# Sandwich block on one core: new per-engine orders of work, another assignment of PSUM banks, other waits

## The reference

```
q, k, v = LN(x) @ Wq.T + bq, LN(x) @ Wk.T + bk, LN(x) @ Wv.T + bv     # 16 heads of 8
q, k = exp(q), exp(k)
num = q . cumsum(k outer v);  den = sum(q * cumsum(k))
x1  = x + LN((num / den) @ Wo.T + bo)
xn  = rms_norm(LN(x1)) * gamma_x;  se = rms_norm(slot_embeds) * gamma_slot   # 512 slots
logits = xn @ se.T
slots  = softmax(logits over tokens).T @ xn
h      = gelu(slots @ w1) @ w2
out    = x1 + LN(softmax(logits over slots) @ h)
```

## Time and profile before

| | us |
|---|---|
| median of 3 runs | 595.33 (594.32 to 596.03) |
| profiled execution, its own time | 594.64 |
| span of the profile | 592.9 |
| PE busy (3772 matmuls) | 557.5, 94% |
| PE weight loads busy | 486.1, 82% |
| DVE busy | 484.2, 82% |
| ACT busy | 473.4, 80% |
| POOL busy | 473.1, 80% |
| mean granted TensorE clock | 0.984 of 2.4 GHz |

### The profile page before, as it was taken

How to read it: one execution, slowest core, us unless ns; L and a number is a source line. 1 busy time by engine, 2 the same in 40 slices (tenths; PEclk the granted TensorE clock), 3 DMA queues, 4 the chain that set the end, 5 groups by cost and what they waited for, 6 DMA issues and landing times.

```text
span 592.9 us, 10573 instructions
## 1 busy us (share of the span) xinstructions
PE 557.5 (94%) x3772; PEld 486.1 (82%) x3772; DVE 484.2 (82%) x922; ACT 473.4 (80%) x1244; POOL 473.1 (80%) x462
## 2 busy tenths in 40 slices
PE   7937999999999999999999999999999999999886
PEld 7925898888888898888888988888888988887775
DVE  4897888888988888888888888889888888878430
ACT  3255889988888889888888899888888888888663
POOL 4777888889888988889888888898888888974100
PEclk9958999999999999999999999999999999999999
DMA  4000000000000000000000000000000000000000
GB/s 115 10 19 19 19 9 19 19 28 28 27 28 28 10 28 18 28 28 28 28 27 28 10 26 20 28 28 28 28 27 12 26 19 28 19 26 10 11 9 19
DMA packets 16825, 14.29 MB, mean 24 GB/s; under 512 B 2850, under 2 KB 16644, under 8 KB 16772
## 3 DMA queue, kind: packets, MB, share of 16 engines
q1 hardware_dynamic: 14708, 12.76, 7.1%
q10 hardware_dynamic: 2064, 0.86, 0.6%
HBM read 5.25 MB, written 4.19 MB: 16 GB/s over the span
## 4 chain that ended last, share of the span: by engine, by line
PE 42%; POOL 23%; ACT 19%; DVE 10%; issue 3%; DMA 1%; SPq 0%; POOLq 0%; DVEq 0%; ACTq 0%
POOL kv_lo L318 11%; PE banks L929 9%; PE banks L955 8%; POOL x_rs L296 7%; ACT kv_hi L422 6%; ACT L430 6%; PE banks L802 5%; PE banks L804 5%; PE banks L803 5%; DVE prod L1253 4%; ACT hid L447 3%; DVE xh L1157 3%; PE banks L782 3%; PE banks L881 2%; ACT disp_t L545 2%
## 5 line engine op out<-in xcount | busy, mean ns | idle before, releaser
L942 PE MATMUL banks<-w_c,hid 128*128 128x128 f32 x1024 | 124.6, 276 | 2.4 <-ACT hid L447 2.4
L942 PEld LDWEIGHTS banks<-w_c,hid 128*128 128x128 f32 x1024 | 119.2, 192 | 3.5 <-ACT hid L447 2.2
L318 POOL TENSOR_TENSOR kv_lo<-kv,kv_hi 128x1152 fp32r<-128x1152 f32 x31 | 81.7, 2636 | 32.5 <-ACT kv_hi L422 32.5
L1253 DVE TENSOR_TENSOR prod<-banks,E 128x768 f32<-128x768 f32 x96 | 88.3, 948 | 1.9 <-PE banks L882 1.9
L1268 DVE TENSOR_REDUCE banks<-prod 128x288 f32<-128x2304 f32 x32 | 81.5, 2545 | 0.0
L212 POOL TENSOR_TENSOR kv_prev<-prev 128x1024 f32<-128x1024 f32 x31 | 66.8, 2153 | 10.5 <-DMA prev<-E 10.5
L955 PEld LDWEIGHTS banks<-proc,comb 128*128 128x128 f32 x512 | 61.1, 191 | 17.0 <-DVE prod L1253 14.9
L380 POOL TENSOR_TENSOR kv<-kv,kv_prev 128x1024 f32<-128x1024 f32 x31 | 74.7, 2410 | 0.0
L447 ACT ACTIVATE hid<-banks 128x512 f32<-128x512 f32 x128 | 70.5, 612 | 4.8 <-PE banks L804 2.0
L212 POOL TENSOR_TENSOR kv<-E 128x1024 f32<-128x1024 f32 x32 | 68.6, 2144 | 4.1 <-ACT E L422 2.2
L1318 DVE TENSOR_REDUCE neg_max<-banks 128x4 f32<-128x1024 f32 x32 | 39.2, 1224 | 31.2 <-PE banks L804 31.2
(11 more groups left out here) (140 smaller groups left out, 1516.9 us busy)
## 6 DMA issues: line engine op xcount, KB each, us to landing
X<-in_L_attn_x_dram SPq DMA_DIRECT2D x32, 128.0 KB, 2.1
out_dram<-res SPq DMA_DIRECT2D x32, 128.0 KB, 2.0
prev<-E SPq DMA_DIRECT2D x32, 112.0 KB, 2.1
w_in<-in_L_ffn_w_dram ACTq DMA_DIRECT2D x2, 256.0 KB, 4.6
prev<-E SPq DMA_DIRECT2D x32, 15.0 KB, 2.0
se_in<-n_L_ffn_slot_embeds_dram ACTq DMA_DIRECT2D x1, 256.0 KB, 3.2
w_in<-in_L_attn_Wq_dram SPq DMA_DIRECT2D x1, 64.0 KB, 2.4
w_in<-in_L_attn_Wk_dram SPq DMA_DIRECT2D x1, 64.0 KB, 2.2
```

The lines of the kernel that those rows point to most:

```text
L318: pool.tensor_tensor(kv_lo[:, :], kv[:, :], kv_hi[:, :].bitcast(F32), ALU.subtract)\
L942: last = pe.matmul(PR[:, j, :], hid[:, f, j * P:(j + 1) * P], w2_c[:, f, :], start=(f == 0), stop=(f == FJ - 1))
L1253: dve.tensor_tensor(prod[u][:, :, d0 * DIM:d1 * DIM].rearrange("p c (d f) -> p c d f", d=g), CU[k].rearrange("p (o d f) -> p o d f", o=1, ...
```

## The change

No operation is added or removed; the lists, the banks and the waits are new.

- **Banks.** The second and third unit of `cumulate` get banks 4 and 0, so no two units share one. The mixture's output moves to 4, the gathered slots to 6, the first transposed dispatch weights to 1, the attention transposes to 6. The four groups of `hidden` go to 5, 2, 5 and 0. Bank 2 is one of the two of the logits.
- **TensorE.** `subtract_max` comes ahead of `cumulate(.., 2)`, `att_transpose` ahead of `project`, `hidden` runs 0, 1, 3, 2. `logits(n)` now waits for gelu 1 of the block before, `project` for gelu 3.
- **SP's queue.** `shift_odd(s - 1)` is issued ahead of `store(s - 8)`.
- **VectorE.** `x_statistics` comes ahead of the two maxima, `x_normalise` ahead of `dispatch_scale`, both residuals behind it; `multiply` runs 2, 1, 0; `xT_low` and `own_sum` come later.
- **ScalarE.** `v_evict` comes ahead of `dispatch_exp`, `combine_exp(.., 0)` ahead of `dispatch_copy`, `slT_high` ahead of `xT_high`, `o_squares` between two gelus.
- **GpSimd.** `x_rstd_of` comes ahead of `sums_low` of the block before, `o_rstd_of` behind it.
- The first blocks are written out anew: `wo_centre` and `x_statistics(3)` come behind the first multiplies, `w2_centre` behind `xnT_high(0)`. PE's and DVE's regular step now reach into the tail.

The diff, cut to its core (of the lists, the regular steps alone):

```diff
@@ banks
-        CU = [banks[:, 6, 0:DU * DIM], banks[:, 5, 0:DU * DIM], banks[:, 5, 0:DU * DIM]]
+        CU = [banks[:, 5, 0:DU * DIM], banks[:, 4, 0:DU * DIM], banks[:, 0, 0:DU * DIM]]
-        AT = banks[:, 7, 0:SEQ]
-        YO = banks[:, 4, 0:NC * YW]
+        AT = banks[:, 6, 0:SEQ]
+        YO = banks[:, 6, 0:NC * YW]
-        DT = [banks[:, 0, :], banks[:, 7, :]]
-        SL = banks[:, 0, :]
-        HP = [banks[:, 6, :], banks[:, 0, :], banks[:, 6, :], banks[:, 4, :]]
+        DT = [banks[:, 1, :], banks[:, 7, :]]
+        SL = banks[:, 6, :]
+        HP = [banks[:, 5, :], banks[:, 2, :], banks[:, 5, :], banks[:, 0, :]]
...
@@ GpSimd, def step(s)
                 x_rstd_of(s)
+                sums_low(s - 2)
+                o_rstd_of(s - 6)
                 y_rstd_of(s - 3)
                 outer_odd(s - 1)
                 x1_rstd_of(s - 3)
                 pair_keys(s - 1)
-                x_negative(s - 2)
+                x_negative(s - 1)
+                own_value(s - 2)
                 outer_even(s - 1)
-                own_value(s - 2)
                 pair_sum(s - 1)
-                o_rstd_of(s - 5)
                 own_product(s - 1)
-                sums_low(s - 1)
@@ ScalarE, def step(s)
                 attT_copy(s - 3)
+                v_evict(s - 1)
                 dispatch_exp(s - 4)
-                v_evict(s - 1)
                 y_squares(s - 3)
                 proc_copy(s - 5)
+                combine_exp(s - 4, 0)
                 dispatch_copy(s - 4, 0)
                 dispatch_copy(s - 4, 1)
                 x1_squares(s - 3)
-                combine_exp(s - 4, 0)
+                slT_high(s - 4)
                 xT_high(s)
-                slT_high(s - 4)
                 combine_exp(s - 4, 1)
                 gelu_table(s - 4)
                 xnT_high(s - 3)
+                gelu(s - 4, 0)
                 o_squares(s - 5)
-                gelu(s - 4, 0)
+                gelu(s - 4, 1)
                 gelu(s - 4, 3)
-                gelu(s - 4, 1)
                 gelu(s - 4, 2)
@@ TensorE, x_transpose
+                after(pe, disp_ready[0], n - 4)
@@ TensorE, project(n, 0)
-                    after(pe, gelu_ready[1], n - 4)
+                    after(pe, gelu_ready[3], n - 4)
+                    pe.wait_ge(xT_lo_ready, n + 1)
@@ TensorE, cumulate(n, 1)
-                    pe.wait_ge(prod_ready[2], n + 1)
+                    if n == 2:
+                        pe.wait_ge(kv_lo_ready, n + 1)
+                    after(pe, res_ready, n - 4)
@@ TensorE, logits
+                after(pe, gelu_ready[1], n - 1)
@@ TensorE, gather_slots
+                after(pe, x1_ready, n + 1)
@@ VectorE, def step(s)
                 x_statistics(s)
+                slot_maxima(s - 4)
+                part_maxima(s - 4)
+                token_maxima(s - 4)
+                x_normalise(s)
+                dispatch_scale(s - 4)
                 second_residual(s - 6)
-                token_maxima(s - 4)
-                own_sum(s - 2)
-                dispatch_scale(s - 4)
-                x_normalise(s)
+                first_residual(s - 3)
                 multiply(s - 2, 2)
-                first_residual(s - 3)
-                multiply(s - 2, 0)
                 multiply(s - 2, 1)
-                xT_low(s)
+                multiply(s - 2, 0)
                 x1_normalise(s - 3)
+                own_sum(s - 2)
                 slT_low(s - 4)
                 attention_sums(s - 2)
                 xnT_low(s - 3)
+                xT_low(s)
                 attention(s - 2)
-                slot_maxima(s - 3)
-                part_maxima(s - 3)
```

More of the change, by code:

```diff
@@ L201, in after @@
+        x_stat = sem("s_xstat")
         def after(eng, s, n):
@@ L676, in first_steps @@
                 xnT_high(4)
+                gelu(3, 0)
                 o_squares(2)
-                gelu(3, 0)
+                gelu(3, 1)
                 gelu(3, 3)
-                gelu(3, 1)
                 gelu(3, 2)
+                exp_table(8)
+                sums_high(6)
+                qk_evict(7)
+                attT_copy(5)
+                v_evict(7)
+                dispatch_exp(4)
+                y_squares(5)
+                proc_copy(3)
+                combine_exp(4, 0)
+                dispatch_copy(4, 0)
+                dispatch_copy(4, 1)
+                x1_squares(5)
+                slT_high(4)
+                xT_high(8)
+                combine_exp(4, 1)
+                gelu_table(4)
+                xnT_high(5)
+                gelu(4, 0)
+                o_squares(3)
+                gelu(4, 1)
+                gelu(4, 3)
+                gelu(4, 2)
+                exp_table(9)
+                sums_high(7)
+                qk_evict(8)
+                attT_copy(6)
+                v_evict(8)
+                dispatch_exp(5)
+                y_squares(6)
+                proc_copy(4)
+                combine_exp(5, 0)
+                dispatch_copy(5, 0)
+                dispatch_copy(5, 1)
+                x1_squares(6)
+                slT_high(5)
+                xT_high(9)
+                combine_exp(5, 1)
+                gelu(5, 0)
+                xnT_high(6)
+                gelu(5, 1)
+                o_squares(4)
+                gelu(5, 3)
+                gelu(5, 2)
             def step(s):
@@ L773, in _ @@
             first_steps()
-            for s in range(8, 33):
+            for s in range(10, 33):
                 step(s)
@@ L1128, in _ @@
             first_steps()
-            for s in range(6, 32):
+            for s in range(6, 34):
                 step(s)
@@ L1363, in first_steps @@
                 x_normalise(2)
+                multiply(0, 2)
                 own_sum(0)
-                multiply(0, 2)
+                multiply(0, 1)
                 multiply(0, 0)
-                multiply(0, 1)
                 xT_low(2)
+                x_statistics(3)
                 attention_sums(0)
+                wo_centre()
                 attention(0)
                 bo_centre()
-                x_statistics(3)
                 slot_low()
                 x_normalise(3)
-                own_sum(1)
@@ new lines, in first_steps @@
+                x_normalise(4)
+                dispatch_scale(0)
+                multiply(2, 1)
+                first_residual(1)
+                multiply(2, 2)
+                multiply(2, 0)
+                x1_normalise(1)
+                own_sum(2)
+                slT_low(0)
+                attention_sums(2)
+                xnT_low(1)
+                xT_low(4)
+                x_statistics(5)
+                attention(2)
+                slot_maxima(1)
+                part_maxima(1)
@@ L1388, in step @@
+                token_maxima(1)
+                x_normalise(5)
+                dispatch_scale(1)
+                first_residual(2)
+                multiply(3, 2)
+                multiply(3, 1)
+                multiply(3, 0)
+                x1_normalise(2)
+                own_sum(3)
+                slT_low(1)
+                attention_sums(3)
+                xT_low(5)
+                xnT_low(2)
+                attention(3)
             def step(s):
                 x_statistics(s)
-                second_residual(s - 6)
```

382 lines of the change are left out of this document (173 added, 209 removed).

## The result

The changed kernel takes **588.33 us** (median of 4 runs, 587.3 to 590.2), the kernel before 595.68 on the same chip (4 runs, 594.32 to 599.38). The ratio is 0.988, 95% interval 0.985 to 0.991: faster by 1.2%. Forecast were 589.6 and a range of 584.5 to 598.0.

What follows compares the result with a forecast made beforehand. The prediction took TensorE as nearly the bound, with waits around x_rs and a shared bank holding the 16.78 us step. Middle -7.2, head +1.5 and tail 0 sum to -5.7, off the 595.33 median: 589.6 us, range 584.5 to 598.

Steps and rivals of the forecast that it cites:

- The step of 16.5 us: Middle of the run: one step falls from 16.77 to 16.5 us, over 27 steps -7.2 us.
- TensorE's own way: Middle step: logits now waits for gelu 1, made second of four; estimated 0 to 0.2 us on the floor.
- the floor: Middle step: 16.28 us, from one early step with TensorE busy throughout; at most 13.2 us to win.
- Way A: Middle step, from dispatch product through gather, gelus and exponentials back to it: 16.39 us, at most 16.52.
- a tenth over A: Middle step: allowance for three ways within 0.15 us waiting for one another, giving 16.5 us.
- The old chain cut twice: Middle step: separate banks for units 1 and 2, and x_rs ahead of kv_lo, take its 1.66 us off the path.
- Way B: Middle step: xh stands still until kv_lo ends, then 0.30 to 0.60 us follow before the product; 16.43 to 16.73 us.
- the lock eats the gain: Rival, middle step: o_rs behind kv_lo keeps VectorE out, product up to 0.27 late; 594.9 us, chance 0.12.
- o_rs caught by the product: Rival, middle step: o_rs starts inside the dispatch product and delays first_residual; step about 17.0, 603 us, chance 0.10.
- SP's queue, costed at nothing: SP's queue: shift issued earlier, ahead of the store; kv_prev gets slack, a late shift cannot lengthen a step.
- The head: Before block 0's gather: work ahead of b_rows on DVE delays it by 0 to 3 us, taken as +1.5.
- The tail: After block 27's gather: same pieces from logits to gather with the same table load; 0, within 1 either way.

Runs made afterwards that it cites:

- `gelu1_first`: The changed kernel with gelu 1 ahead of o_squares in ScalarE's regular step; 585.45 us, ratio 0.984 to the kernel before.
- `xT_first`: The changed kernel with xT_high ahead of slT_high again in ScalarE's regular step; 585.27 us, ratio 0.984 to the kernel before.
- `both`: The changed kernel with gelu 1 ahead of o_squares and xT_high ahead of slT_high; 586.7 us, ratio 0.984 to the kernel before.
- `before_xrs`: The kernel before with only x_statistics and x_rstd_of a place earlier, ahead of the maxima and kv_lo; 590.22 us, ratio 0.992.
- `xh_behind_head`: The changed kernel with x_normalise behind dispatch_scale and, in the head, x_statistics(3) later on VectorE; 589.1 us, ratio 0.989 to the kernel before.
- `both_store`: The changed kernel with gelu 1 ahead of o_squares, xT_high ahead of slT_high, and SP's store ahead of the shift; 584.99 us, ratio 0.981.
- `v_behind`: The changed kernel with v_evict behind dispatch_exp again in ScalarE's regular step; 629.1 us, ratio 1.058 to the kernel before.
- `before_xrs_v`: The kernel before with x_statistics and x_rstd_of earlier and v_evict ahead of dispatch_exp, no bank changed; 581.62 us, ratio 0.976.

## Why the prediction was right

**The step of 16.5 us.** Right to 0.01 (16.50), and with it the term of -7.2 (-7.27).

**What sets it.** Here the ranking failed. The prediction put the way through the exponentials first, with 16.39, and TensorE's own way, "0 to 0.2 us on the floor", "below A or level with it". The trace shows room on Way A behind the product (0.24, where 0.06 is enough) and a stall of 0.16 at logits; `gelu1_first` takes 0.14 off the step by that stall alone. The 0.07 at the gather is on the last piece of Way A, but it comes from TensorE's own order: from the transposes' start to the end of the copies it takes 1.73 (303.02 to 304.75) and 0.14 more to the gather, and what TensorE has to do meanwhile fills only 1.80. The prediction had named this wait as a sign ("TensorE now and then for the disp copies"); it is there in every step but the last. `gelu1_first`, `xT_first` and `both` stop at 16.36 or 16.37, 0.08 above the floor, which is what this wait would explain; no run takes it away alone. The 16.5 came from "a tenth over A", an allowance for three ways near one another. So the number was in part luck: the way that filled it was the one ranked last, though its size, 0.23 on the floor, is near the "0 to 0.2" that it was given.

**The old chain cut twice.** Both cuts exist, but the prediction did not ask which of them was needed. The early x_rs alone ends TensorE's wait for the bank (`before_xrs`), and so the bank costs nothing in the old order once x_rs is early. The step that failed is the reading of x_rs's 1.66 us. The prediction knew that 0.95 of it was the product's doing, and used this row for a rival, but counted the eviction of v only as 0.26 us added to Way A. It was the cheapest cure for just that meeting. Alone it gives 12.6 us where the whole change gives 7.3. The sign of it lay in the prediction's own floor: it took the early step of 16.28 as one "in which nothing is left out" and did not ask what sets it apart, which is v ahead of the exponentials.

**Way B and the lock.** The signs came as named: xh takes 1.04 us for the pair and ends 0.33 behind kv_lo, o_rs takes 0.70. The forecast for Way B, 16.43 to 16.73, cannot be told from 16.51, since the exponentials end at the same time (`xh_behind_head`). The rival "the lock eats the gain" did not happen: o_rs at 301.05 did not hold xh's second half, and the product started at 301.56.

**o_rs caught by the product.** Not o_rs but y_rs was caught, 1.51 for 0.71. The rival's point of decision was right (o_rs gets through if it starts ahead of the product, here 0.51 ahead), and y_rs's loss lies beside the second residual. The rival's price was added wrongly: its own terms, 4.39 + 1.23 + 1.31 + 4.3 + 5.99, make 17.2 and not 17.0, which would be some 609 us and not 603.

**SP's queue, costed at nothing.** "kv_prev gets slack" is right (its DMA waits are gone from the list). That a shift which comes late "can then no longer lengthen a step" is wrong for the queue: what is late now is the store behind it. It costs 1.7 us (`both` against `both_store`), and 26.5 us as soon as v comes late (`v_behind`). The move of v pays for the move of the shift.

**The head**, +1.5, came as +1.44, and the changed order of TensorE's first attention as named: bias rows at 36.98 instead of 34.65, +2.3. The slow tensor_scalar on b_row was not spared: it still started inside kv_lo (33.76, kv_lo from 32.90 to 35.52) and took 1.84 us, 1.71 before.

**The tail**, 0 within 1, came as -1.46, outside its bound. This is the term that the prediction left at nothing. The last steps are 16.03, 15.99 and 15.72 us; in the kernel before they were 16.49, 17.31 and 15.45, so most of the gain is in the 17.31 that became 15.99. Which edit of the tail's lists does it was not tested. It makes nearly all of the 1.6 us between the forecast sum of -5.7 and the -7.3 of the spans. That it takes back the head's +1.44 was not foreseen.

## What to carry to other kernels

Where a tiny operation on the path takes more than twice its time because it starts just inside a large one on the shared port, it is enough to swap who comes first. Delaying the large one, if it has slack, frees the small one as well as hastening the small one does, and may be a move of one line on a third engine. Where one step of a regular run is shorter than all others, find out what is different in it before calling it the floor: here the difference was the better kernel. After a reordering that pays, try its parts alone on the old kernel: here one moved line is worth nearly twice the whole change. And on an in-order queue, what stands behind a waiting transfer inherits its wait: put first what is ready.

## What the hardware showed that was not expected

Two rows stand for the sharing between VectorE and GpSimd. A power of 128x2 that starts inside a product of 128x1024 ends 0.55 to 0.57 us behind the product's end, in three kernels: x_rs at 303.65 in the kernel before, y_rs at 301.83 in the changed one, and here in `before_xrs_v`:

```profile
313.55 1.23 DVE L1332 TENSOR_TENSOR disp_t<-disp_t,disp_inv 128x1024 f32<-128x1024 f32 x1
313.90 1.43 POOL L334 TENSOR_TENSOR y_rs<-y_ve,minus_half 128x2 f32<-128x2 f32 x1 [0.74 <-ACT y_sq L465]
```

The other way round nothing was held. A power that starts only 0.03 ahead of the product takes its 0.70, and the product 1.24 (102.22 and 102.25 in the kernel before). The same power takes 0.70 beside xh's second half (301.05 in the changed kernel), which takes its 0.33, and in the kernel before 0.71 beside a pair of 0.60. The Trainium skill (SBUF — State Buffer, "Who interferes with whom") states that the one which issues second is shut out for the whole of the first. The waiting xh and y_rs agree with it; VectorE beside a power that has just started does not. And x_rs took 0.71 from 297.00 on although the reduction neg_max, which reads PSUM, had run on VectorE since 296.79 for 1.23 us; so not all of VectorE's operations hold it.

TensorE's granted clock in the head is the other. Between 40 and 50 us it is 0.51 in the changed kernel and 0.58 in the kernel before, near the lower level of 1.2 GHz, after waits of 2 to 4 us between short pieces of work. From 50 to 60 it was 1.00 in the changed kernel's profile, but 0.84 in `xh_behind_head` and 0.79 in `both`. The head of `both` has the same order of work as the changed kernel's. Its first gather came 1.2 us later (58.82), although its first attention transposes started 1.0 us sooner (32.37 against 33.41). So the longer low clock costs some 2 us from there on. The profiles of the changed kernel and the kernel before were alike in this, and +1.44 holds for such a pair; in other executions the head can cost 1 us more.
